# A graph network in four layers on one core: the record scatters paced by TensorE and moved between stages, and the softmax divided by a logarithm

## The reference

```
x = ln(x + L0(x))   # mean of x[dst] over the edges of src, then two matrices with relu
x = ln(x + L1(x))   # attention: q[dst] * (k[src] + e) per head, softmax over the edges of a node,
                    # sum of (v[src] + e) * alpha, skip, two matrices with gelu
x = ln(x + L2(x))   # (x + 3 * sum of weight * x[dst]) / 4 over the edges of src
x = ln(x + L3(x))   # a matrix per relation and direction, summed over edges forwards and backwards
```

```
ex = exp(alpha - max);  alpha = ex / (sum(ex) + 1e-16)
```

## Time and profile before

| | us |
|---|---|
| median of 3 runs | 4655.66 |
| lowest, highest | 4649.19, 4657.07 |
| span of the profiled execution (first to last instruction) | 4651.0 |
| busy: POOL, PE, DVE, ACT | 3414.1, 2871.3, 2230.8, 613.9 |

### The profile page before, as it was taken

One profiled execution on the slowest core, in us unless ns is written; L12 is line 12 of the kernel. 1 busy time (PEld: TensorE's weight loads), 2 busy tenths in 40 slices (PEclk: granted clock), 3 DMA queues, 4 the chain that ended last, 5 costly groups with the idle time before them and its releaser, 6 DMA issues. The chain is left out here.

```text
span 4651.0 us, 50018 instructions
## 1 busy us (share of the span) xinstructions
PE 2871.3 (62%) x13750; PEld 2210.0 (48%) x13751; DVE 2230.8 (48%) x2711; ACT 613.9 (13%) x1076; POOL 3414.1 (73%) x3213
## 2 busy tenths in 40 slices
PE   3799998967777777751989643444444333333333
PEld 1688887943333333331989433333333333333333
DVE  7899997656666666668971621111111111111112
ACT  0355554010000000001751000000000000000000
POOL 1888886857777777767867677777777777777775
PEclk8899999968877878875999866666666566555556
DMA  6466566816666666651989523222222122212221
GB/s 191 139 189 183 170 187 209 265 37 172 170 170 170 170 171 173 173 153 59 278 241 276 174 68 94 68 68 68 68 68 68 49 53 52 53 53 53 53 53 51
DMA packets 498663, 599.91 MB, mean 129 GB/s; under 512 B 190115, under 2 KB 367441, under 8 KB 496248
## 3 DMA queue, kind: packets, MB, share of 16 engines
q0 software_dynamic: 117856, 246.12, 19.4%
q1 hardware_dynamic: 337751, 229.77, 17.7%
q10 hardware_dynamic: 42944, 122.68, 7.3%
HBM read 406.69 MB, written 204.36 MB: 131 GB/s over the span
## 5 line engine op out<-in xcount | busy, mean ns | idle before, releaser
L1151 PE MATMUL ps<-got,g_hot 128*128 x3224 | 719.2, 414 | 1151.3 <-DMA got<-y_back,s_msg 597.5
L721 POOL DMA_INDIRECT rec_by_src<-rec,pos x782 | 1123.9, 1437 | 344.1 <-issue 245.8
L1151 PEld LDWEIGHTS ps<-got,g_hot 128*128 128x128 f32 x3224 | 667.8, 316 | 1213.1 <-issue 1213.1
L1612 POOL DMA_INDIRECT sc_kv<-kv,d_src x806 | 762.0, 945 | 254.9 <-issue 245.3
L1036 POOL DMA_INDIRECT got<-y_forward,d_msg x782 | 739.1, 945 | 238.2 <-issue 238.2
L1036 POOL DMA_INDIRECT got<-y_back,s_msg x766 | 722.7, 943 | 241.7 <-issue 233.1
L806 PE MATMUL ps<-ln_low,ln_hot 128*125 128x256 f32 x2848 | 618.9, 380 | 19.7 <-DVE ln_low L783 15.9
L806 PEld LDWEIGHTS ps<-ln_low,ln_hot 128*125 128x125 f32 x2848 | 535.3, 188 | 103.2 <-issue 22.7
L1059 DVE TENSOR_TENSOR g_hot<-ps,src_loc 128x1024 f32<-128x1024 f32 x101 | 123.4, 1224 | 832.1 <-PE ps L1151 831.7
L1715 PE MATMUL ps<-q,sc_hotT 128*128 x1616 | 274.2, 322 | 236.4 <-DVE sc_hotT L1657 207.4
L1067 DVE TENSOR_TENSOR g_y<-ps,ms_b 128x384 f32<-128x384 f32 x75 | 41.8, 558 | 732.1 <-PE ps L1164 732.1
(11 more groups left out here) (328 smaller groups left out, 3102.4 us busy)
## 6 DMA issues: line engine op xcount, KB each, us to landing
linked<-ln_out SPq DMA_DIRECT2D x320, 224.0 KB
ve<-sc_kve ACTq DMA_DIRECT2D x202, 256.0 KB
wv_ve<-ve SPq DMA_DIRECT2D x101, 512.0 KB, 5.0
l_links<-linked SPq DMA_DIRECT2D x25, 800.0 KB, 7.3
l_links<-linked ACTq DMA_DIRECT2D x25, 800.0 KB, 9.2
attr_pairs<-ln_feats POOLq DMA_DIRECT2D x7, 2048.0 KB
sc_attr<-attr_pairs SPq DMA_DIRECT2D x202, 64.0 KB, 2.6
sc_kv<-kv,d_src POOLq DMA_INDIRECT x806, 3.0
```

The costliest lines, as they stand in the source:

```text
L721: pool.indirect_dma_start(out=dram["rec_by_src"], out_offset=bass.IndirectOffsetOnAxis(ap=S["pos"][:, c:c + 1], axis=0), in_=S["rec"][:, c ...
L1151: last = pe.matmul(ps[:, bass.ds(columns[j], width)], hot[:, q, j, :], got[:, bass.ds(slots[j], width)], start=False, stop=True, skip_grou ...
L1612: pool.indirect_dma_start(out=kv[:, q, j, :], out_offset=None, in_=dram["kv"], in_offset=bass.IndirectOffsetOnAxis(ap=S["d_src"][:, c:c + ...
```

## The change

RECORD_PARTS is set anew: index 6 to 24, link 302 to 312, l0 stays 70, m0 30 to 25, project 22 to 15, maxima 82 to 88, weigh 100 to 106, the second linked sum 118 to 104 (one part now, "second"), norm 52 to 38.

```
-RECORD_PARTS = {"index": 6, "link": 302, "l0": 70, "m0": 30, "project": 22, "maxima": 82, "weigh": 100, "m1": 42, "l2": 76, "norm": 0}
+RECORD_PARTS = {"index": 24, "link": 312, "l0": 70, "m0": 25, "project": 15, "maxima": 88, "weigh": 106, "second": 104, "norm": 0}
```

index_stage sends 10 tiles ahead of the gathers and 14 (LATER) behind them, and writes the -1 ahead of `node` here instead of in the softmax stage:

```
+            if send is not None:
+                first, last = part_of(send)
+                send_some(pool, S, dram, first, last - LATER)
             for k, s in enumerate(stairs):
                 pool.wait_ge(tiled, k + 1)
...
             if send is not None:
-                send_records(pool, S, dram, send)
+                send_some(pool, S, dram, last - LATER, last)
...
+            sp.wait_ge(fronted, 1)
+            sp.dma_start(dram["node"][0:1].rearrange("(a n) -> a n", a=1), front[:, :]).then_inc(begun, 16)
```

mlp_layer, project and norm_and_messages send their tiles behind waits for the progress of TensorE or VectorE:

```
+            for c in range(CHUNKS):
+                for sem, some in ((turned, each - 2 * (each // 3)), (hidden, each // 3), (product, each // 3)):
+                    pool.wait_ge(sem, c + 1)
+                    pool.nop(nofuse=True)
+                    send_some(pool, S, dram, sent, min(sent + some, last_sent))
...
+            first, last = part_of("project")
+            for n in range(last - first):
+                pool.wait_ge(product, max(1, n * BLOCKS // (last - first)))
...
+            first, last = part_of("norm")
+            for n in range(last - first):
+                if n:
+                    pool.wait_ge(biased, n * BLOCKS * PIECES // (last - first))
...
+            pool.wait_ge(S["sent"], 16 * TILES)
```

The second linked sum sends 4 tiles at once and 100 behind marks, four a block:

```
+    EASE_AT = (1, 7, 13, 19)
...
+            first, last = part_of("second")
+            free = last - first - BLOCKS * EASE
+            send_some(pool, S, dram, first, first + free)
+            for n in range(BLOCKS * EASE):
+                pool.wait_ge(eased, n + 1)
+                pool.nop(nofuse=True)
+                send_some(pool, S, dram, first + free + n, first + free + n + 1)
...
+                    if k in EASE_AT:
+                        last.then_inc(eased, 1)
```

scores issues the four loads of `node` and `loc` at its 25th step on SyncE's queue; their tiles and their semaphore now live from project on:

```
+                if n == 4 * WAYS:
+                    for name, a in (("before", dram["node"][0:rows]), ("node", dram["node"][1:1 + rows]), ("after", dram["node"][2:2 + rows]),
+                                    ("place", dram["loc"].rearrange("b e -> (b e)")[0:rows])):
+                        sp.dma_start(S["mx_" + name][:, :], a.rearrange("(p c) -> p c", p=P)).then_inc(S["noded"], 16)
```

The softmax stage loses these loads and the division:

```
-                act.activation(score[:, h, :], score[:, h, :], ACT.Exp).then_inc(exped, 1)
+                act.activation(back[:, h, :], score[:, h, :], ACT.Exp).then_inc(exped, 1)
+            for h in range(HEADS):
+                act.wait_ge(summed, h + 1)
+                act.activation(back[:, h, :], back[:, h, :], ACT.Ln, bias=guard[:, 0:1]).then_inc(logged, 1)
+            for h in range(HEADS):
+                act.wait_ge(weighted, h + 1)
+                act.activation(score[:, h, :], score[:, h, :], ACT.Exp).then_inc(shared, 1)
...
-                link(dve.tensor_scalar_add(back[:, h, :], back[:, h, :], 1e-16))
-                link(dve.reciprocal(back[:, h, :], back[:, h, :]))
-                dve.tensor_tensor(score[:, h, :], score[:, h, :], back[:, h, :], ALU.mult).then_inc(shared, 1)
-            dve.wait_ge(shared, HEADS)
+                dve.engine_nop().then_inc(summed, 1)
+            for h in range(HEADS):
+                dve.wait_ge(logged, h + 1)
+                dve.tensor_tensor(score[:, h, :], score[:, h, :], back[:, h, :], ALU.subtract).then_inc(weighted, 1)
+            dve.wait_ge(weighted, HEADS)
```

More of the change, by code:

```diff
@@ L439, in index_stage @@
         below = m.sb(tag + "_below", [P, TILES])
+        front = m.sb(tag + "_front", [1, 1])
+        fronted, begun = m.sem(tag + "_fronted"), m.sem(tag + "_begun")
+        LATER = 14
         ready, spread, tiled, stepped, flipped, listed = (m.sem(tag + n) for n in (
@@ L488, in _ @@
             sp.wait_ge(filed, 16 * len(stairs))
+            sp.wait_ge(begun, 16)
             if sent:
@@ L1285, in _ @@
         def _(pool):
-            send_records(pool, S, dram, tag)
+            sent, last_sent = part_of(tag)
+            each = -(-(last_sent - sent) // CHUNKS)
+            for c in range(CHUNKS):
[3 more added lines that the diff above has]
+                    send_some(pool, S, dram, sent, min(sent + some, last_sent))
+                    sent = min(sent + some, last_sent)
         @block.tensor
@@ L1500, in _ @@
         def _(pool):
-            send_records(pool, S, dram, "project")
+            first, last = part_of("project")
+            for n in range(last - first):
+                pool.wait_ge(product, max(1, n * BLOCKS // (last - first)))
+                pool.nop(nofuse=True)
+                send_some(pool, S, dram, first + n, first + n + 1)
         @block.scalar
@@ L1744, in softmax_maxima @@
         turn = m.sb("mx_turn", [P, HR, P])
[L1745 to L1748, removed]
+        node, node_b, node_a, loc = (S["mx_" + name] for name in ("node", "before", "after", "place"))
         bad = m.sb("mx_bad", [P, L])
@@ L1814, in _ @@
         def _(sp):
-            sp.wait_ge(fronted, 1)
-            sp.dma_start(dram["node"][0:1].rearrange("(a n) -> a n", a=1), front[:, :]).then_inc(stored, 16)
-            sp.wait_ge(stored, 16)
-            for t, a in ((node_b, dram["node"][0:P * L]), (node, dram["node"][1:1 + P * L]),
-                         (node_a, dram["node"][2:2 + P * L]), (loc, flat_loc[0:P * L])):
-                sp.dma_start(t[:, :], a.rearrange("(p c) -> p c", p=P)).then_inc(noded, 16)
             for h in range(HEADS):
@@ L1824, in _ @@
                              turn[:, h * PAIR_BLOCKS:(h + 1) * PAIR_BLOCKS, :]).then_inc(stored, 16)
-            sp.wait_ge(stored, 16 * (1 + HEADS))
+            sp.wait_ge(stored, 16 * HEADS)
             for h in range(HEADS):
@@ L1838, in _ @@
             link = Chain(dve, order)
-            dve.memset(front[:, :], -1.0).then_inc(fronted, 1)
-            dve.wait_ge(noded, 16 * 4)
+            dve.wait_ge(S["noded"], 16 * 4)
+            link(dve.memset(guard[:, :], 1e-16))
             link(dve.tensor_scalar(bad[:, :], loc[:, :], 0.0, None, ALU.is_lt))
@@ L1901, in _ @@
             dve.wait_ge(exped, HEADS)
-            carried(2, False, same, score, top, 0.0, ALU.mult, ALU.add)
+            carried(2, False, same, back, top, 0.0, ALU.mult, ALU.add)
             for h in range(HEADS):
@@ L2105, in _ @@
         def _(pool):
-            send_records(pool, S, dram, "norm")
+            first, last = part_of("norm")
+            for n in range(last - first):
+                if n:
+                    pool.wait_ge(biased, n * BLOCKS * PIECES // (last - first))
+                    pool.nop(nofuse=True)
+                send_some(pool, S, dram, first + n, first + n + 1)
+            pool.wait_ge(S["sent"], 16 * TILES)
         @block.scalar
@@ L2286, in gnn_kernel @@
             S["alpha"] = a.sb("alpha_cols", [P, HEADS, PAIR_COLS])
+            for name in ("before", "node", "after", "place"):
+                S["mx_" + name] = a.sb("mx_" + name, [P, PAIRS_PAD])
+            S["noded"] = a.sem("mx_noded")
             with ExitStack() as early:
```

11 lines of the change are left out of this document (6 added, 5 removed).

## The result

The changed kernel takes 4682.44 us (median of 4 runs, 4681.97 to 4683.66) against 4654.26 for the kernel before (4649.19 to 4657.07, now 4 runs): a ratio of 1.0064, 95% interval 1.0050 to 1.0078. It is slower by 28 us; 14 were forecast, and the range ended at 4680. The span is 4680.2 us, 29.2 more than before.

What follows compares the result with a forecast made beforehand. The prediction bounded each stage by its last engine: GpSimd in scores, VectorE's chain in softmax, TensorE in the second linked sum. +7 - 1 + 7.5 + 0.5 = +14 us gave 4670 us, range 4648 to 4680.

Steps and rivals of the forecast that it cites:

- Index, +7: Index stage: eight more scatters behind the gathers end at 149.6, so link starts 6.5 to 7.7 us later; +7 taken.
- the idle time is its slack plus a microsecond or two of stage change: Stage ends: GpSimd's idle time before its next first DMA read as slack, 4.9 us in index, 25.5 in link.
- Softmax, -1: Softmax stage: other engines finish 18 us earlier, but GpSimd's 88 scatters end at 2194.1 and hide it; -1, bounds -18 to +13.
- Second linked sum, +7.5: Second linked sum: the stall recurs with 15 scatters left, ending at 2575.6 against TensorE's 2568.1; +7.5, up to +9.
- I read it as one event, a full path for descriptors: Second linked sum: GpSimd's 9.85 us stop and SyncE's 9.88 us issue of the biases load share one cause.
- rival 1: Second linked sum: the stall does not come again, so +6.5 in all, 4662 us; chance 0.32 together with another rival.
- Norm, +0.5: Norm stage: the last scatter waits for piece 73 of 75 and lands about with y's last store; +0.5, -1 to +2.
- Link, 0: Link stage: ten more scatters at 1.27 to 1.65 us fit into 25.5 us of slack; 0.
- weigh, 0: Weigh stage: six more scatters take at most 10 us within 21.9 us of idle time; 0.
- Early loads and logarithm: Softmax stage: early loads start the maxima some 5 us sooner; with the logarithm, everything but GpSimd is done 18 us earlier.
- Rival 2: Stage ends do not wait for GpSimd: index costs 0, softmax gives 18, second linked sum 0; 4638 us; chance 0.04.
- The doubt about the rates in the softmax stage: Softmax stage: scatters may run free at 1.27 us instead of 1.65, giving -18 there, 4645 us; chance 0.11.

Runs made afterwards that it cites:

- experiment 9: Scatters of softmax, second linked sum, norm and 22 of weigh sent in two separate stages of 126, the second with a wait halfway; 4954.15 us beside 4654.25.
- experiment 6: Kernel with counts laid out by the drain and no marks (64 scatters in softmax), but reciprocals in place of the logarithm; 4639.45 us, ratio 0.9976.
- experiment 5: Changed kernel's softmax, early loads and row of -1, without marks, counts laid out by the drain (64 scatters in softmax); 4623.40 us against 4650.92 for the kernel before.
- the first of 8: Kernel laid out by the drain, without marks, with 60 instead of 64 scatters in softmax and 51 instead of 47 in norm; 4622.03 us, ratio 0.9933.
- experiment 1: Changed kernel with the 88 softmax scatters moved behind it into three stages of their own (8, 20, 60); 4769.73 us, before 4657.53.
- experiment 2: Changed kernel without marks in the second linked sum, its 104 scatters sent freely; 4684.42 us, ratio 1.0052 to the kernel before.
- the changed kernel again: Changed kernel unaltered, measured again beside its version without any marks; 4684.03 us, ratio 1.0070 to the kernel before.
- experiment 10: Changed kernel with the second linked sum's 104 scatters still paced, but the last mark in block 20 of 25; 4678.27 us, ratio 1.0050 to the kernel before.
- experiment 4: Kernel before with the new softmax arithmetic (logarithm), early loads and early row of -1, scatter counts and pace unchanged; 4657.55 us, ratio 1.0000.
- experiment 3: Changed kernel without the waits before norm's 38 scatters; 4684.83 us, ratio 1.0060 to the kernel before.
- experiment 8: Kernel laid out by the drain with 60 softmax scatters and 51 in norm, 4622.03 us; then also with the four loads late again, 4627.73 us.

## Why the prediction was wrong

*Index, +7: +9.8 measured.* The last scatter was forecast for 149.6 and came at 149.63. The step that failed is the next one, "the idle time is its slack plus a microsecond or two of stage change". I took the 4.86 us of the earlier trace rows at 144.27 for slack and two other stage changes for the price. They are, but for 0.9 us, GpSimd's own drain, 3.9 us before and 3.6 after. So there was no slack into which a later scatter could go.

*Softmax, -1: +6.7.* GpSimd was forecast to send its last 132 us into the stage and did at 133.6. The others were done after 107.0, sooner than the 115 I gave them. The mis-sized term is again what stands between the last scatter and the stage's end: 7.5 us, of which 7.2 are the drain, taken as 1.4.

*Second linked sum, +7.5: +7.9, for another reason.* "I read it as one event, a full path for descriptors" is the step that failed: the stall comes behind the 113th scatter, with or without SyncE, as experiment 9 shows. In the five other traces with 118 the ends of stall and issue lay 0.4 to 2.8 us apart, so the 0.3 us of the earlier trace rows were chance. With 104 scatters no stall came. The rest of rival 1, "its scatter ends at 2568: 0", was right on the scatter and missed the 8.5 us of drain behind it. Two errors cancelled, so the right number here was luck.

*Norm, +0.5: +6.3.* The last scatter was issued by 2666.28 and all had landed at 2669.7, with SyncE's last store. Then came the DRAIN of 3.15 us, which before lay beside the stores, as the last free scatter ended 8 us before the stage did. The other 3 us are 1.4 of VectorE ending later and 1.5 of later landing of y. The granted clock of TensorE moves norm too. The 25 us in the middle of it, in experiments 6 and 5, both without waits (columns as in the earlier trace rows, the clock is the third number from the end):

```profile
2575.90:2600.90 25.00, 19.87 (x71) 11.74 (x71) 22.58 (x66) 2.54 (x5) 19.19 (x20) 1.00 0.57 207
```
```profile
2561.60:2586.60 25.00, 19.86 (x66) 11.38 (x65) 21.50 (x62) 2.53 (x5) 19.21 (x20) 0.93 0.52 188
```

Without waits norm took 75.8 to 76.5 us in the seven traces with 1.00 there and 79 in the two with 0.93 (5 and the first of 8). With waits it took 80.8 and 82.4 at 1.00 (experiment 1 and the changed kernel) and 82.9, 83.0 and 88.3 at 0.93 (2, the changed kernel again, 10). So at the same clock the waits cost 4 to 6 us, and 9 in experiment 10. Why the clock falls in some executions is open.

*Link, 0: +1.5, and weigh, 0: +2.0.* GpSimd's part in link grew from 615 to 637 us. A scatter there took 2.0 us on average (615 us for 309 DMAs), not 1.27 to 1.65, so the ten are some 20; experiment 4, with 302 as before, took 622. With the drain the 25.5 us of idle time were used up, and GpSimd ended the stage by 3.3 us. In weigh the others were done at 2411.1 and GpSimd's drain behind 106 at 2413.5; but weigh took 201.1 to 204.9 us over all traces with 100 to 106 scatters, so its 2.0 can't be told from the spread.

*Early loads and logarithm.* "Some 5 us" for the loads: 4.3. For both I gave 18 us off the other engines' part: it was 26 in the changed kernel and 25 in experiment 4. The logarithm's share was 13 in my sum and 20.7 in experiments 5 and 6, of which 16 reached the stage. So the loads were right and the arithmetic too small, and both were hidden, as forecast.

With the drains put into my own sum, everything else as it stood, index by its measured 3.6 and the others by the line of experiment 3: index 149.6 + 3.6 gives +9.8, softmax 2194.1 + 7.2 gives +5, second (no stall) 2568 + 8.5 gives +8, norm 2644.9 + 3.15 gives +3.3, in all 26 us. Measured: 28.2. Rival 2 fell, and so did its ground: "GpSimd was never last at a stage with scatters" was false in index, l0 and softmax. The drains stood in the trace of before. These 26 were worked out afterwards, with a line fitted to these runs; experiments 5 and 8 are forecasts that counted on such a drain.

The doubt about the rates in the softmax stage is half settled: alone, scatters go at 1.26 us (experiment 1), and 88 of them in the softmax stage at 133.6 / 88 = 1.52. That VectorE's work is what slows them was not tried by itself; in link they went at 2.0, in weigh at 1.84.

## What to carry to other kernels

A block is over when every engine's queue has drained, and for GpSimd that can be microseconds behind its last visible instruction: read the drains at each stage's end before calling idle time slack. Background work on an engine should end early rather than run evenly; pacing by marks up to the last one puts the drain on the path. A saving on the other engines is worth only what the background count beside it leaves room for, so set the count after the saving, not before.

## What the hardware showed

- GpSimd's DRAIN at the end of a stage took 0.034 + 0.082 us for each scatter sent since the stage began, whether free or paced, and after all had landed: 3152 ns behind 38, 3887 behind 47, 4213 behind 51, 4295 behind 52. Beside busy DMA engines (a share of 0.87 to 1.02 while it drained) it was longer: 10.8 us behind 84 in experiment 9, 11 to 15 us behind 104. Behind link's 302 to 312 scatters it was only 4.1 to 5.7 us, and behind the 805 gathers of the first gather_sum 7.7 us, with which it ended that stage in every trace. The Trainium skill (VectorE: DVE Perf Modes, The DRAIN you can't avoid) tells, beside VectorE's own, of a DRAIN of about 12 ns, constant on all five engines, from the start and end of the program. Whether those at the end of a stage are of that kind, no run here shows. In the kernel before 14 of VectorE's 18 took 10 to 24 ns, which is near it, and link's took 2.2 us; GpSimd's are far from it.
- GpSimd stopped behind the 113th scatter of a stage in every trace in which that many followed each other with no gather between: 3.0 us alone, 8 to 10 us beside table loads. 806 gathers in a row in scores brought no stop of that size, and left a drain of 3.8 to 4.8 us. What it waits for there is open. So is what held GpSimd's drain in the index stage with 4 or 6 scatters behind the gathers: in six traces it ended 1.4 to 1.6 us behind SyncE's last work, whenever the last scatter had come.
- Scores and the two gather_sum stages, which are bound by GpSimd's gathers, differed by up to 6 us each between executions of the same code (1022 to 1028, 1982 to 1988 us). A difference of 8 us in one stage had to be read there; in all it was lost in this.
